# Preparing the ternary and output weights of a gated cross-attention block: two blocks of instructions against one

## The reference

```python
def ternarize(W, threshold):                 # threshold 0.05
    absW = jnp.abs(W)
    delta = threshold * jnp.max(absW)
    mask = absW > delta
    n = jnp.maximum(jnp.sum(mask), 1)
    alpha = jnp.sum(jnp.where(mask, absW, 0.0)) / n
    Wt = alpha * jnp.sign(W) * mask
...
h = gelu(x @ Wq1.T + b1)                     # W1 is 2048 x 512
y = h @ Wq2.T + b2                           # W2 is 512 x 2048
...
out = out @ w_o.T + b_o                      # attention's output, w_o is 512 x 512
```

## Time and profile before

| | us |
|---|---|
| Median of 3 runs | 3619.79 (3611.29 to 3620.09) |
| The profiled execution | 3634.41, its span 3632.6 |
| `ternarize` in the span | 2801.28 to 2916.39 |
| `po` in the span | 2916.39 to 2926.88 |
| `residual`, then `feed_forward`, `quantize` | 2926.88 to 3632.6 |

### The profile page before, as it was taken

One profiled execution on the slowest core, in us unless ns is written; L12 is line 12 of the kernel. 1 busy time (PEld: TensorE's weight loads), 2 busy tenths in 40 slices (PEclk: granted clock), 3 DMA queues, 4 the chain that ended last, 5 costly groups with the idle time before them and its releaser, 6 DMA issues. The chain is left out here.

```text
span 3632.6 us, 54033 instructions
## 1 busy us (share of the span) xinstructions
PE 3253.3 (90%) x18048; PEld 1722.2 (47%) x18048; DVE 2280.4 (63%) x3692; ACT 1519.0 (42%) x2141; POOL 96.5 (3%) x98
## 2 busy tenths in 40 slices
PE   6999999994999999999999999999996168999992
PEld 5777777773333333333333333333331146777771
DVE  5666666663467676676766767666662967343435
ACT  3433443331355555555555555555544034222222
POOL 0000000000000000000000000000000044000000
PEclk8999999996599999999999999999988579999996
DMA  5777777769353544525345353544521055000005
GB/s 151 162 163 167 165 164 164 167 157 123 64 121 71 113 98 86 120 64 123 88 96 110 74 123 76 108 101 83 122 51 61 41 151 145 1 1 0 0 1 185
DMA packets 369886, 368.54 MB, mean 101 GB/s; under 512 B 42288, under 2 KB 292208, under 8 KB 369272
## 3 DMA queue, kind: packets, MB, share of 16 engines
q1 hardware_dynamic: 365576, 359.05, 44.2%
q10 hardware_dynamic: 4224, 8.39, 0.6%
HBM read 246.21 MB, written 121.15 MB: 101 GB/s over the span
## 5 line engine op out<-in xcount | busy, mean ns | idle before, releaser
L834 ACT ACTIVATE at_probs<-at_st 128x1024 f32<-128x1024 f32 (+1 forms) x832 | 851.1, 1023 | 880.7 <-PE at_st L713 875.2
L862 DVE TENSOR_REDUCE at_cm<-at_mx 128x2 f32<-128x896 f32 x768 | 822.1, 1089 | 460.5 <-PE at_mx L729 460.5
L713 PE MATMUL at_st<-at_qst,at_kst 101*128 101x512 f32 (+1 forms) x1664 | 616.5, 452 | 19.2 <-ACT at_probs L834 18.9
L713 PEld LDWEIGHTS at_st<-at_qst,at_kst 101*128 101x128 f32 (+1 forms) x1664 | 245.3, 187 | 737.5 <-ACT at_probs L834 648.6
L752 PE MATMUL at_acc<-at_probs,at_vt 128*32 128x512 f32 (+2 forms) x3584 | 483.6, 614 | 21.8 <-ACT at_ev L815 21.6
L764 PE MATMUL at_acc<-at_probs,at_ones 128*32 128x512 f32 (+2 forms) x3584 | 483.1, 614 | 0.0
L729 PE MATMUL at_mx<-at_kmx,at_qmx 33*128 33x448 f32 (+1 forms) x2048 | 382.8, 426 | 46.3 <-DMA at_kmx<-stack_rows 36.3
L729 PEld LDWEIGHTS at_mx<-at_kmx,at_qmx 33*128 33x128 f32 x2048 | 171.7, 191 | 301.5 <-issue 246.6
L862 DVE TENSOR_REDUCE at_top<-at_mx 128x2 f32<-128x514 f32 x256 | 176.9, 691 | 125.9 <-PE at_mx L729 120.9
L1295 ACT ACTIVATE ff_h<-ff_psa,ff_b1c,alpha 128x512 f32<-128x512 f32 x128 | 99.4, 778 | 344.2 <-PE ff_psa L1272 344.2
L879 DVE RECIPROCAL at_rl<-at_ev 128x512 f32<-128x512 f32 x64 | 210.1, 3324 | 49.3 <-ACT at_ev L815 49.3
(11 more groups left out here) (184 smaller groups left out, 3981.3 us busy)
## 6 DMA issues: line engine op xcount, KB each, us to landing
at_kst<-k_high SPq DMA_DIRECT2D x256, 200.1 KB
at_kmx<-k_high SPq DMA_DIRECT2D x64, 400.2 KB
at_kst<-k_low SPq DMA_DIRECT2D x128, 200.1 KB
pj_xin<-in_ctx_dram SPq DMA_DIRECT2D x96, 256.0 KB, 4.5
k_high<-pj_kh SPq DMA_DIRECT2D x96, 256.0 KB, 3.5
k_low<-pj_kl SPq DMA_DIRECT2D x96, 256.0 KB, 5.2
values<-pj_vs SPq DMA_DIRECT2D x96, 256.0 KB, 5.0
at_vt<-values SPq DMA_DIRECT2D x32, 768.0 KB
```

The lines of the kernel that those rows point to most:

```text
L713: pe.matmul(st[0:kn, h % 2, :], kst[p][:, h, t * P:t * P + kn], qst[p][:, h, :], start=True, stop=True).then_inc(S["st_done"], 1)
L834: act.activation(probs[0:kn, SLOT[t], 2 * run:2 * run + 2, :], st[0:kn, :, :], ACT.Exp, scale=SCALE).then_inc(S["exp_done"], 2)
L862: dve.tensor_reduce(dst, mx[:, 2 * slot:2 * slot + 2, 0:kn], AX.X, ALU.max).then_inc(S["mx_free"], 1)
```

## The change

- One block prepares W1, W2 and `w_o`. The second `prepare_weights` is gone, with its load, its identity and its block's end; `ident` of the first block is used for `w_o`.
- W1 and W2 are loaded in four pieces of 1 MB each (128 x 4 x 512), each with a semaphore of its own, in the order W1, `w_o`, W2. They go into the tile `xy`, which is allocated earlier for this and is otherwise first written by `residual`.
- DVE takes each piece's largest magnitude as it lands (W1), or between other work (W2).
- `below` and `tern` work on a whole piece, 2048 elements a partition, in place of a tile of 512: 8 of each for both matrices.
- `prod` is gone. ACT computes, for each piece, `Relu(w - delta)` and `Relu(-w - delta)` with accumulators; `alpha`'s numerator is their sum plus the count times `delta`.
- Rows are assigned to partitions and pieces in such a way that the transposes of a piece need that piece alone. PE turns each piece as its levels are there, in two banks of 8 transposes.
- ACT copies all 16 of those banks, 1024 elements a partition each; DVE copies none.
- The order on each engine is written out, as below.

```diff
+        srcs = (w1.rearrange("(s o p) i -> p s o i", p=P, o=4), w2.rearrange("(o p) (s i) -> p s o i", p=P, i=D))
+        piece = lambda w, s: nat[:, 16 * w + 4 * s:16 * w + 4 * s + 4, :]
...
+            def largest(w, s):
+                dve.wait_ge(w_in[w][s], 16)
+                dve.tensor_reduce(top[:, w, 4 * s:4 * s + 4], piece(w, s), AX.X, ALU.max,
+                                  apply_absolute_value=True).then_inc(S["rowmax"], 1)
...
+            def three_levels(w, s):
+                n = 4 * w + s
+                if n >= 2:
+                    dve.wait_ge(S["t_done"], n - 1)
+                dve.tensor_scalar(below[n % 2][:], piece(w, s), m[:, w, 3:4], 0.0, ALU.is_lt, ALU.add,
+                                  accum_out=sums[:, w, 0, s:s + 1]).then_inc(S["below_done"], 1)
+                dve.wait_ge(S["below_done"], n + 1)
+                if n >= 3:
+                    dve.wait_ge(S["turned"], 2 * (n - 2) + (4 if n >= 7 else 0))
+                dve.scalar_tensor_tensor(tern[n % 3][:], piece(w, s), m[:, w, 2:3], below[n % 2][:], ALU.is_gt, ALU.subtract,
+                                         accum_out=sums[:, w, 1, s:s + 1]).then_inc(S["t_done"], 1)
...
+            for s in range(4):
+                largest(0, s)
+            row_largest(0)
+            threshold(0)
+            three_levels(0, 0)
+            three_levels(0, 1)
+            largest(1, 0)
+            largest(1, 1)
+            three_levels(0, 2)
+            three_levels(0, 3)
+            largest(1, 2)
+            largest(1, 3)
+            row_largest(1)
+            for c in range(NG):
+                low_weights(c)
+            threshold(1)
+            for s in range(4):
+                three_levels(1, s)
+            for w in range(2):
+                add_up(w)
...
+            def beyond(w, s):
+                n = 4 * w + s
+                if s == 0:
+                    act.wait_ge(S["step"], 2 * w + 2)
+                for r, sign in enumerate((1.0, -1.0)):
+                    if 2 * n + r >= 2:
+                        act.wait_ge(S["over_done"], 2 * n + r - 1)
+                    act.activation(over[r][:], piece(w, s), ACT.Relu, bias=m[:, w, 3:4], scale=sign,
+                                   accum_out=sums[:, w, 2 + r, s:s + 1]).then_inc(S["over_done"], 1)
+
+            def evacuate(w, s):
                 for half in range(2):
-                    last = act.activation(dst(n, half), bank(n, half), ACT.Copy)
-                last.then_inc(S["evac0"], 1)
+                    k = bank_of(w, s, half)
+                    act.wait_ge(S["turned"], k + 1)
+                    act.activation(dst(w, s, half), ps[:, k % 8, :].bitcast(BF16).rearrange("p (r d) -> p r d", r=2),
+                                   ACT.Copy).then_inc(S["evacuated"], 1)
+
+            for s in range(4):
+                beyond(0, s)
+                if s:
+                    evacuate(0, s - 1)
+            evacuate(0, 3)
+            for c in range(NG):
+                act.wait_ge(S["turned"], 8 + c + 1)
+                act.activation(wo[0][:, c, :], ps[:, c, :], ACT.Copy).then_inc(S["evacuated"], 1)
+            for s in range(4):
+                beyond(1, s)
+                if s:
+                    evacuate(1, s - 1)
+            evacuate(1, 3)
...
-            ternarize(nc, w1, w2, t1, t2, alpha)
             xy = ctx.enter_context(nc.sbuf_tensor("xy", [P, B * QT, D], F32))
             with ExitStack() as inner:
                 wo = tuple(inner.enter_context(nc.sbuf_tensor(f"wo_{s}", [P, NG, D], F32R)) for s in ("high", "low"))
-                prepare_weights(nc, ident, [w_o], [wo], "po")
+                ternarize(nc, ident, w1, w2, w_o, t1, t2, alpha, wo, xy)
```

More of the change, by code:

```diff
@@ L1098, in layer_norm_rstd, with ternarize @@
     return L[:, 4:5]
-def ternarize(nc, w1, w2, t1, t2, alpha):
-    NT = 16
+def ternarize(nc, ident, w1, w2, w_o, t1, t2, alpha, wo, nat):
+    NT = 4
     with ExitStack() as ctx:
         a = Names(nc, ctx, "tw")
[L1107 to L1110, removed]
+        nato = a.sb("nato", [P, NG, D])
+        below = [a.sb(f"below{p}", [P, NT, D], BF16) for p in range(2)]
+        tern = [a.sb(f"tern{p}", [P, NT, D], BF16) for p in range(3)]
+        over = [a.sb(f"over{p}", [P, NT, D]) for p in range(2)]
@@ L1119, in ternarize @@
         S = {n: a.sem(n) for n in names}
-        w_in = [a.sem(f"w_in{w}") for w in range(2)]
+        w_in = [[a.sem(f"w_in{w}{p}") for p in range(4)] for w in range(2)]
+        o_in = a.sem("o_in")
         block = ctx.enter_context(nc.Block())
[L1122 to L1132, removed]
+        srcs = (w1.rearrange("(s o p) i -> p s o i", p=P, o=4), w2.rearrange("(o p) (s i) -> p s o i", p=P, i=D))
@@ L1134, in _, with dst @@
+        piece = lambda w, s: nat[:, 16 * w + 4 * s:16 * w + 4 * s + 4, :]
+        PIECES = [(w, s) for w in range(2) for s in range(4)]
+        bank_of = lambda w, s, half: 8 * w + 2 * s + half + (4 if w else 0)
+        def dst(w, s, half):
+            if w == 0:
+                return t1[:, 2 * half:2 * half + 2, s * D:(s + 1) * D]
+            return t2[:, 4 * s + 2 * half:4 * s + 2 * half + 2, :]
         @block.sync
         def _(sp):
-            sp.dma_start(nat[0][:], srcs[0]).then_inc(w_in[0], 16)
@@ L1186, in _ @@
                 dve.reciprocal(m[:, w, 6:7], m[:, w, 5:6]).then_inc(S["a_step"], 1)
-                dve.wait_ge(S["a_step"], b + 3)
-                dve.tensor_tensor(alpha[:, w:w + 1], total[:, w, 2:3], m[:, w, 6:7], ALU.mult).then_inc(S["a_step"], 1)
-            for n in range(8, 16):
-                dve.wait_ge(S["turned"], n + 1)
-                for half in range(2):
-                    last = dve.tensor_copy(dst(n, half), bank(n, half))
-                last.then_inc(S["evac1"], 1)
+                dve.wait_ge(S["a_step"], b + 5)
@@ new lines, in turn @@
+            def turn(w, s):
+                n = 4 * w + s
+                pe.wait_ge(S["t_done"], n + 1)
+                for half in range(2):
+                    k = bank_of(w, s, half)
+                    free(k)
+                    for r in range(2):
+                        for q in range(4):
+                            at = r * D + q * P
+                            last = pe.transpose(ps[:, k % 8, :].bitcast(BF16)[:, at:at + P],
+                                                tern[n % 3][:, q, (2 * half + r) * P:(2 * half + r + 1) * P], identb[:])
+                    last.then_inc(S["turned"], 1)
```

89 lines of the change are left out of this document (43 added, 46 removed).

## The result

| | before | after |
|---|---|---|
| Median, runs of the same chips | 3617.31 us (3611.29 to 3620.09, 4 runs) | 3579.53 us (3562.86 to 3587.13, 4 runs) |
| Ratio, 95% interval | | 0.9887 (0.9853 to 0.9922) |
| Profiled execution, its span | 3634.41, 3632.6 | 3587.13, 3585.0 |
| Preparing W1, W2 and `w_o` | 125.58 us | 71.67 us |
| `attend` | 1925.76 us | 1932.22 us |

The kernel is faster, by 1.1% in these runs. The block that was forecast at 71.6 us takes 71.67; the median, forecast at 3565.8 us, came at 3579.5, 1.5 us above the range. (The median of before has one run more than it had ahead of the prediction.) So the sum for the block was right, and what was allowed for the scatter of the runs was too little; the experiments are about both.

A forecast was written before the change was run, and what follows sets the result against it. The serial preparing blocks (125.6 us), mostly DVE, bound their stretch; 13.9 + 3.3 + 27.9 + 2.4 + 23.7 + 0.4 = 71.6 us saves 54.0 us: 3619.8 - 54.0 = 3565.8 us, range 3556 to 3578.

The forecast's parts named there:

- `low_weights` and W2's threshold: Between W1's and W2's halves: DVE waits 2.15 us for ACT, then W2's threshold takes 0.25; counted as 2.4 us.
- Pieces: Block's start: 1 MB loads land 2.7 us apart, the first at 5.5 us, W1's last taken at 13.9.
- Wide pairs: DVE, both halves: `below` and `tern` over 2048 elements take 4.67 us a piece, 18.7 for four.
- Relu with its read: ACT, both halves: one Relu plus its accumulator read costs 1.95 to 2.3 us, taken as 2.05.
- Copies: ACT, W2's half: each bank copy of 1024 elements takes 0.91 us.
- Who is last: W2's half: ACT sets the end, 23.7 us against DVE's 18.7 for four pieces.
- Magnitudes to ACT: W2's half: 23.7 us with Relus on ACT against 27.9 with wide `prod` on DVE, so 4 us shorter.
- POOL after a pause: Block's start: POOL may need some 8 us; first asked 16 us in, so nothing counted; without that cover, up to 8.
- Dear pieces: Rival, loads of W1 and W2: each piece pays its 5.5 us alone, 9.7 us more, 3575.5 us; chance 0.06.
- Engines in turn: Rival, W2's half: ACT and DVE take turns on the same piece, 18.7 + 23.7 us, giving 3584.5; chance 0.08.
- Relu of 2.6: Rival, ACT: a Relu with its read costs 2.6 us or more; at 2.6, W2's half 4.4 longer, 3570; chance 0.02.
- `residual` at half clock: Rival, after the block: PE's clock stays low, up to +97 us, 3663; chance 0.03, plus 0.02 for about eating the gain.

## Why the prediction was right, and where it failed

**The block.** Each term of the sum beside what the timeline gives (borders 2807.58, 2822.16, 2825.46, 2853.18, 2855.72, 2878.99, 2879.25):

| term | predicted | measured |
|---|---|---|
| last piece of W1 there | 13.9 | 14.58 |
| last `largest`, POOL, threshold | 3.3 | 3.30 |
| DVE, W1's half and W2's `largest` | 27.9 | 27.72 |
| `low_weights` and W2's threshold | 2.4 | 2.54 |
| ACT, W2's half | 23.7 | 23.27 |
| block's end | 0.4 | 0.26 |
| sum | 71.6 | 71.67 |

- *Pieces.* Off by 0.7 us in this execution and by nothing in the second (13.88): 2.7 us apart came from the five loads of `pw`; here they were 2.7 to 3.1 apart, and the first landed at 5.9 instead of 5.5. That the sum of all terms agrees to 0.1 us is thus partly luck: the landing was 0.7 late and W2's half 0.4 short.
- *Wide pairs.* 4.67 us each, as derived: 2867.44 - 2862.78 = 4.66 between two `tern`s.
- *Relu with its read.* 1.99 us, between my 1.95 and 2.3, below the 2.05 that I took. The read lasts 190 ns, but the next Relu starts 0.09 us after the read does. Here the page "ScalarE: Activation LUTs" of the Trainium skill, section "What ACT_TABLE_LOAD costs", which no row of before could bear out, is borne out: 280 ns + 0.833 ns x 2048 = 1986 ns against 1994 ns measured.
- *Copies.* 0.91 us predicted, 3.75 / 4 = 0.94 measured, and 0.9 as a step between two.
- *Who is last.* ACT, as said; with no magnitudes at all the block is 2.1 us shorter, so ACT ends W2's half only a little after DVE would, and the two are nearly even. (Before the change ACT was not quite idle beside DVE's tiles, as the prediction says: it had 8.05 of 70.94 us.)
- *Magnitudes to ACT.* The prediction put this move at 4 us, W2's half alone. Undone, it costs 15.9: in W1's half DVE sets the time, and four operations of 2.29 us, 9.2 in all, come back there too. The prediction left that half out; the forecast does not rest on it, and the expectation of 85 to 88 us counted it.
- *POOL after a pause.* I counted nothing for the 8.7 us of `quantize`; the step from the small maximum to the threshold took 0.55 us. That came out, and whether the 16 us of cover are what saved it was not tested.

**The rivals.** Dear pieces: 0.1 to 1.1 us instead of 9.7. (The prediction has it that by the rule for large transfers the time would be this rival's; the rule asks for at least 1 MiB, which the pieces meet, and puts no 5.5 us on each.) Engines in turn: no operation longer by more than 1 ns on average. Relu of 2.6: 1.99. `residual` at half clock: 144.25 us, 1.5 less than before; the clock recovers there as it did.

**Where the gain comes from.** Undone one at a time, the parts cost, by the rest behind W1's landing: magnitudes to ACT 16.4, merge with `po` 8.5, width 8.0 us; and pieces, with their own landing, 5.6. They add up to 38.5 of 53.9. The other 15.4 us belong to what was not undone alone: mainly that transposes need one piece, so that W2's copies end with the work and not behind it (11.36 us before, the fourth line of the earlier trace rows), and to parts that lean on each other. How they divide is only argued, since no kernel was run with the old order of the transposes.

**The step that failed.** It is a size in the step from the sum to the runs: "the three runs of before lie within 9 us, so either median can be off by some 4 to 6", and with it the upper end of 3578. Three runs within 9 us looked like a narrow scatter; 70 executions of before in this study have a standard deviation of 12.4 us (in part from chip to chip), ten of after 11.4. With that a median of four is off by some 6 to 7 us, and the difference of two by 9 (an estimate from those deviations). The base was right: 3619.8, the median of three, against a mean of 3620.0 us over the 70, so taking the gain off the median and not off the slower profiled execution was right too. But three runs did not warrant that, and the agreement was luck. The first median of after, 3579.5, was a high draw; the second was 3567.5, 1.7 us from the forecast, which was luck as well. In the first four runs of after the profiled execution was again the slowest, by 7.6 us against their median; in the second batches of both kernels it was not, so that distance is no property of a profiled execution.

By means (3620.0 and 3572.0 us) the gain is 48.1 us, with 7.7 us either side at 95%; the 54 us of the trace lie within. Whether the missing 6 us are scatter or something that one profile in each kernel does not show stays open.

I had read the row that told of the scatter, PE busy 39.5 of 40 us at a clock of 0.50 in `attend`, and used it only for the rival on `residual`. A stretch where PE is at work but at half speed, and whose end no row ties to an event, was the place to ask how long it might be in the next execution. The block was off by 0.1 us and the median by 13.7: 7.5 of these are between the first median and the mean of ten executions, 3572.0, and the other 6.2 are less than that mean's own uncertainty of 7.

## What to carry to other kernels

Cut a serial block at the events that release engines (last load, threshold, last bank), add each stage from rows of the same operations elsewhere in the kernel, and a new block can be forecast to about a microsecond; here each term came within 0.7 us. Ask in each stage which engine is then last. Before giving a range for a median out of three runs, look for stretches whose length may differ from run to run, here TensorE busy at half clock, since such a one is both the error of the forecast and a gain left lying. Compare variants worth less than that scatter by the block's length in the trace, not by their medians, and count from where its loads have landed: here the rest repeated to 0.01 us, where the loads moved by 0.8.

## What the hardware showed

- TensorE stayed at a granted clock of 0.50 and 0.51 (1.2 GHz) for 57 and 72 us while busy 55 and 70 us of them, with the many small matmuls of `attend`, and went to 1.00 (2.4 GHz) at a time that differed by up to 57 us between executions of the same code of `attend`, and by 17 to 19 between two of the same kernel. What ends the stretch was not found. In each of the three profiles with 16 matmuls of 96 x 128 x 512 in a row it rose before these had ended; in one it fell again behind a wait of 1.94 us, and with that wait and the next filled it stayed. The page "TensorE: Matmul & The Clock Gate" of the Trainium skill, in its Part 1, says that the number of slow matmuls differs from run to run and puts the penalty of the ramp under 1% of a typical kernel. Here 57 to 72 us at 0.43 are 25 to 31 us (an estimate, 0.43 us being what `attend` lengthens by for each us of the stretch), 0.7 to 0.9% of the span: that agrees, and it is still as much as half of what this change was to bring.
- In the third stage of the new block, 2.71 us, the clock was 1.00 as well, at the end of the transposes of W1's last piece and the 16 fp32 ones of `w_o`, and in the next, of light work, it was 0.51 on the mean.
- ACT's Relus cost DVE's comparisons on the same fp32 data nothing: 2352 ns with and without.
- Four loads of 1 MB on one queue were there 13.88 to 14.67 us after the first was issued (nine executions), one of 4 MB after 13.62 to 13.83 (three).
